# Cross-attention of a perceiver block: scores with the keys on the partitions

## The chip, the cores and the metric

The kernel runs on one core of one Trainium2 chip. The metric is the time of one execution on the device in microseconds (us). A core has five engines that run side by side, each through its own list in order: TensorE (PE: matmuls; weight loads are shown apart as PEld), VectorE (DVE), ScalarE (ACT), GpSimd (POOL), and SyncE (SP), which here only issues DMAs. They wait for each other through semaphores.

## The reference, cut to what matters

The block is a cross-attention, a self-attention and a mixture of experts, each with a layernorm before and a residual sum behind it. Only the first is touched:

```
x: (4, 256, 256)          ctx: (4, 4096, 256)
h       = layernorm(x)
queries = h @ Wq.T + bq
keys    = ctx @ Wk.T + bk
values  = ctx @ Wv.T + bv
scores  = einsum('bqc,bkc->bqk', queries, keys) / 16
attn    = softmax(scores, axis=-1)          # over 4096 keys
attended= einsum('bqk,bkc->bqc', attn, values)
x       = x + (h + attended) @ Wo.T + bo
```

All is float32.

## The kernel before, in words

The weights are folded: `qk` is h times (Wq.T Wk), so the scores are `qk` times the context itself, and the sum over keys mixes the raw context (`mix`); the value and output weights come behind it. A constant per query, `qbk`, remains of the biases. For accuracy each float32 operand of the large matmuls is split in a high part (a cast to fp32r) and a low part (the original less the high part), and three products are summed: high by high, low by high, high by low.

A batch has 256 queries (two tiles q of 128, `QT`) and 4096 keys, in eight chunks of 512 (`NCH`, `CH`; four tiles j of 128, `J`). The work is a pipeline of two stages over batches: in each of four passes the kernel computes the scores of one batch chunk by chunk, and beside them the probabilities and the mixing of the batch before. Pass 1 has only the first half, passes 2 to 4 have both, and a tail behind them has only the second. Pass 2 starts near 60 us, each full pass takes 65.9.

The list of each engine is written out by hand, by functions called once for each chunk c. In a chunk of a full pass:

- PE: `score` (12 matmuls of 512 columns, queries on the partitions of the result), `transpose_ctx` of the next chunk (8 transposes, L299), `mix` of the batch before (24 matmuls of 256 columns, L342 to L344), `transpose_probs` (8 transposes, L324).
- ACT: `ctx_turned_high` (casts the turned context to `ctxT_hi`, L494), `exps` (exponential of the stored scores, with the sum over keys as a by-product, L508), `probs_high` (casts turned probabilities to `pT_hi`, L517).
- DVE: `scores_out` (PSUM to SBUF, adds `qbk`, takes the maximum of the row as a by-product, L629), `ctx_low` (L614), `ctx_high` (casts the context as it came to `ctx_hi`, L622), `probs_low` (L637).
- POOL: `split`, the low part `ctx_lo` of the context as it came (L247). It needs `ctx_hi`. Its end frees one of four slots of `ctx_stage` for the load of the chunk four further on (L200, SP).

The maximum over all keys of a batch must be known before its first exponential, so `maxima` stands at the end of a pass; `invert_sums` and `normalise` close a batch. The queries of the next batch (`queries`), the product with the output weights (`product`), the statistics of the next layernorm and its scaling are spread over the chunks of a pass. The bias sum on `x_sb` (L261, POOL) is done once, in pass 2.

Of the kernel before, what the change touches and what calls it, by code (L numbers as in the profile page):

```python
# [100 lines left out]
def cross_attention(nc, x_sb, x_stats, x_mv, ident, kept, x, ctx, Wq, bq, Wk, bk, Wv, bv, Wo, bo,  # L101
# [3 lines left out]
    ATT_SCALE = 16 ** -0.5  # L105
    with ExitStack() as st:
# [122 lines left out]
        def _(pool):  # L229
            nc.gpsimd.memset(ident[:], 0.0).then_inc(ident_ok, 1)  # L230
            nc.gpsimd.memset(power[:], -0.5).then_inc(pow_g, 1)
# [8 lines left out]
            def split(b, c):  # L240
                cols = slice(c * J * D, (c + 1) * J * D)
# [5 lines left out]
                nc.gpsimd.tensor_tensor(ctx_lo[:, cols], ctx_in_sb[:, c % SLOTS, :], ctx_hi[:, cols].bitcast(F32),  # L247
                                        ALU.subtract).then_inc(split_g, 1)

            def second_scale(e):  # L250
                tiles = slice(QT * e, QT * (e + 1))
                pool.wait_ge(ve2_v, e + 1)
                nc.gpsimd.tensor_tensor(rstd2[:, tiles], ve2[:, tiles], power[:, tiles], ALU.pow).then_inc(rstd2_g, 1)

            for b in range(B):
                for c in range(NCH):
                    split(b, c)
                    if (b, c) == (1, 1):
# [1633 lines left out]
```

## Time and profile before

| | us |
|---|---|
| median of 3 runs | 674.49 (672.59 to 676.24) |
| the profiled execution | 672.18 |
| its span, first to last instruction | 670.4 |
| PE busy | 598.2 |
| DVE busy | 402.1 |
| ACT busy | 348.1 |
| POOL busy | 249.6 |
| mean granted TensorE clock | 0.964 of full |

A busy share is a mean over stages. A slice is a fortieth of the span, 16.8 us; a digit is its busy share in tenths. In a timeline a row gives the start, the time from start to end (of several instructions together, where it ends in x2 or more), engine, line, operation, result and inputs with their shapes, and in brackets the idle time of the engine before it and who ended it. Matmuls are pipelined: one is shown as 0.28 us long, while the next starts 0.12 later.

### The profile page before, as it was taken

How to read it: one execution, taken by the hardware profiler on the slowest of the kernel's cores; microseconds unless marked ns; L12 is line 12 of the kernel's file. 1: busy time of each engine (PE TensorE's matmuls, PEld its weight loads, DVE VectorE, ACT ScalarE, POOL GpSimd, SP SyncE). 2: the span in 40 equal slices, each digit the busy share in tenths (PEclk: the TensorE clock that was granted, in tenths of full speed). 3: DMA queues.
4: the chain of work that ended last, by engine and by line, in shares of the span. 5: the costliest groups of instructions: out<-in, count | busy, mean ns of one | idle time of the engine just before them, and what ended most of it. 6: DMA issues, size and time to landing. Idle time of an engine off the chain costs nothing. (4 is left out here: it accounts for less than half of the span.)

```text
span 670.4 us, 10668 instructions
## 1 busy us (share of the span) xinstructions
PE 598.2 (89%) x3740; PEld 475.4 (71%) x3740; DVE 402.1 (60%) x794; ACT 348.1 (52%) x1047; POOL 249.6 (37%) x201
## 2 busy tenths in 40 slices
PE   5998999999999998997887867999999876769998
PEld 4887998899989987975555546555558652448887
DVE  3766566666667664336477777699995378335000
ACT  2545444444444435632787861579996366751210
POOL 1352262233223232022696770133546149155000
PEclk8999999999999999999797999999999996699999
DMA  7122012102211220019993000300006147680000
GB/s 258 64 95 94 32 65 94 64 32 82 77 65 36 93 77 0 2 58 171 196 204 127 0 1 4 124 0 0 1 1 137 51 127 236 202 254 8 17 17 23
DMA packets 41586, 53.48 MB, mean 80 GB/s; under 512 B 3649, under 2 KB 37057, under 8 KB 41409
## 3 DMA queue, kind: packets, MB, share of 16 engines
q1 hardware_dynamic: 41536, 52.84, 28.7%
q8 instruction: 29, 0.48, 0.3%
q14 instruction: 21, 0.16, 0.1%
HBM read 48.63 MB, written 4.19 MB: 79 GB/s over the span
## 5 line engine op out<-in xcount | busy, mean ns | idle before, releaser
L247 POOL TENSOR_TENSOR ctx_lo<-ctx_stage,ctx_hi 128x1024 fp32r<-128x1024 f32 x32 | 76.3, 2387 | 157.3 <-DVE ctx_hi L622 135.8
L637 DVE TENSOR_TENSOR pT_lo<-ps,pT_hi 128x512 fp32r<-128x512 f32 x64 | 41.2, 686 | 60.0 <-ACT pT_hi L517 60.0
L342 PE MATMUL ps<-ctx_hi,pT_hi 128*128 128x256 f32 x256 | 75.2, 294 | 1.5 <-DVE pT_lo L637 1.4
L343 PE MATMUL ps<-ctx_lo,pT_hi 128*128 128x256 f32 x256 | 72.4, 283 | 0.0
L344 PE MATMUL ps<-ctx_hi,pT_lo 128*128 128x256 f32 x256 | 72.4, 283 | 0.0
L494 ACT CAST ctxT_hi<-ps 128x512 fp32r<-128x512 f32 x64 | 34.6, 593 | 62.7 <-PE ps L299 62.5
L1688 ACT ACTIVATE comb<-comb,cneg 128x64 f32<-128x64 f32 x160 | 62.9, 401 | 0.0
L629 DVE TENSOR_SCALAR_CACHE_REDUCE scores<-ps,qbk 128x512 f32<-128x512 f32 x64 | 47.5, 750 | 21.2 <-PE ps L311 21.2
L1574 PE MATMUL pf<-phiT,h3T 128*128 128x512 f32 x128 | 60.2, 591 | 0.0
L1659 PE MATMUL pf<-phiT,comb 128*128 128x256 f32 x256 | 56.2, 379 | 0.0
L508 ACT ACTIVATE probs<-scores,negmax 128x512 f32<-128x512 f32 x64 | 46.0, 728 | 16.3 <-DVE rowsum L648 16.3
L517 ACT CAST pT_hi<-ps 128x512 fp32r<-128x512 f32 x64 | 34.3, 589 | 36.6 <-PE ps L324 36.6
L1512 POOL TENSOR_TENSOR disp<-disp,dinv 128x512 f32<-128x512 f32 x32 | 33.6, 1049 | 52.7 <-DVE dinv L1765 52.7
L1659 PEld LDWEIGHTS pf<-phiT,comb 128*128 128x128 f32 x256 | 48.2, 190 | 6.8 <-issue 0.4
L342 PEld LDWEIGHTS ps<-ctx_hi,pT_hi 128*128 128x128 f32 x256 | 49.0, 191 | 2.4 <-DVE pT_lo L637 2.2
L343 PEld LDWEIGHTS ps<-ctx_lo,pT_hi 128*128 128x128 f32 x256 | 49.1, 192 | 0.1
L344 PEld LDWEIGHTS ps<-ctx_hi,pT_lo 128*128 128x128 f32 x256 | 49.0, 191 | 0.0
L614 DVE TENSOR_TENSOR ctxT_lo<-ps,ctxT_hi 128x512 fp32r<-128x512 f32 x64 | 41.2, 685 | 7.5 <-ACT ctxT_hi L494 7.1
L1523 POOL TENSOR_TENSOR comb<-comb,cinv 128x512 f32<-128x512 f32 x32 | 39.9, 1271 | 14.1 <-DVE cinv L1778 14.1
L311 PE MATMUL ps<-ctxT_hi,qk_hi 128*128 128x512 f32 x128 | 42.3, 411 | 2.8 <-issue 2.0
L311 PE MATMUL ps<-ctxT_hi,qk_lo 128*128 128x512 f32 x128 | 39.8, 392 | 0.0
L311 PE MATMUL ps<-ctxT_lo,qk_hi 128*128 128x512 f32 x128 | 39.7, 391 | 0.0
(204 smaller groups left out, 1368.3 us busy)
## 6 DMA issues: line engine op xcount, KB each, us to landing
ctx_stage<-in_ctx_dram SPq DMA_DIRECT2D x32, 512.0 KB, 3.3
w_more<-in_L_ffn_expert_w_dram SPq DMA_DIRECT2D x11, 1024.0 KB, 5.4
h3T<-in_L_ffn_expert_w_dram SPq DMA_DIRECT2D x5, 1024.0 KB, 5.3
qk_parts_dram<-qk_parts SPq DMA_DIRECT2D x8, 384.0 KB, 5.3
q_rows<-qk_parts_dram SPq DMA_DIRECT2D x24, 128.0 KB, 6.5
disp<-qk_parts_dram SPq DMA_DIRECT2D x24, 128.0 KB, 5.8
disp<-in_L_ffn_phi_w_dram SPq DMA_DIRECT2D x1, 2048.0 KB, 8.2
phiT<-in_L_ffn_expert_b_dram SPq DMA_DIRECT2D x4, 512.0 KB, 10.0
```

Of the source, the lines that this page charges most:

```text
L247: nc.gpsimd.tensor_tensor(ctx_lo[:, cols], ctx_in_sb[:, c % SLOTS, :], ctx_hi[:, cols].bitcast(F32), ALU.subtract).then_inc(split_g, 1)
L311: last = nc.tensor.matmul(pS[q][:], a[:, dh, q * P:(q + 1) * P], k[:, c % 2, dh, :], start=step == 0, stop=step == 5)
L342: nc.tensor.matmul(pO[q][:, 0:D], pT_hi[:, c % 2, q, cols], hi, start=c == 0 and j == 0, stop=False)
L343: nc.tensor.matmul(pO[q][:, 0:D], pT_hi[:, c % 2, q, cols], lo, start=False, stop=False)
L344: last = nc.tensor.matmul(pO[q][:, 0:D], pT_lo[:, c % 2, q, cols], hi, start=False, stop=c == NCH - 1 and j == J - 1)
L508: nc.scalar.activation(probs[:, c % 2, q, :], scores[:, q, c * CH:(c + 1) * CH], ACT.Exp, bias=negmax[:, q:q + 1], scale=SCALE, accum_out= ...
L614: nc.vector.tensor_tensor(ctxT_lo[:, c % 2, dh, :], ctx_banks(c, alone)[dh][:], ctxT_hi[:, c % 2, dh, :].bitcast(F32), ALU.subtract).then_ ...
L629: nc.vector.tensor_scalar(scores[:, q, c * CH:(c + 1) * CH], pS[q][:], qbk[:, b * QT + q:b * QT + q + 1], None, ALU.add, ALU.max, accum_ou ...
L637: nc.vector.tensor_tensor(pT_lo[:, c % 2, q, :], probs_banks(c, alone)[q][:], pT_hi[:, c % 2, q, :].bitcast(F32), ALU.subtract).then_inc(p ...
L1574: last = nc.tensor.matmul(psL[u % 4][:], hT[:, c, t * P:(t + 1) * P], phiT[:, c, cols], start=False, stop=c == DH - 1)
L1659: last = nc.tensor.matmul(psY[t][:, 0:HID], comb[:, t, s * P:(s + 1) * P], mixed[:, s, :], start=s == 0, stop=s == ST - 1)
L1688: nc.scalar.activation(column, column, ACT.Exp, bias=cneg[:, c, p:p + 1], accum_out=csum[:, c, p:p + 1]).then_inc(cslot_a, 1)
```

## The change

The scores are computed with the keys on the partitions: the turned context is the stationary operand and `qk` the moving one, four key tiles of 256 queries each, 24 matmuls of 256 columns in a chunk. The probabilities then come out in the layout in which `mix` takes them as the stationary operand, and `transpose_probs` goes.

The maximum over keys now runs over partitions. `running_maximum` (DVE, two of 512 elements a chunk, from PSUM) keeps the elementwise maximum in `running`; at the end of a pass `fold` halves it, `transpose_maxima` (PE) turns it, `shifts` (DVE) reduces it, adds `qbk` and takes the difference, and widens it; `spread_shift` (PE) and `shift_out` (ACT) lay the shift of each query along the free dimension of all partitions, as `shift`. Scores are copied to SBUF by ACT (`scores_out`, two copies of 512 a chunk, a ring of nine chunks in `turned_scores`). POOL adds the shift in place (`subtract`, 1024 elements a chunk). ACT takes the exponential in place (1024 elements) and casts it to `p_hi` (1024), and DVE takes `p_lo` from `turned_scores` and `p_hi`, both in SBUF (1024).

The sums over keys come from two columns of ones behind each 256 columns of `ctx_hi`, so that `mix` has 258 columns in two of three products, and `normalise` takes the reciprocal from PSUM. The PSUM banks are dealt out anew: two pairs for the scores, one for the turned context. `split` of a chunk is put off to two chunks later in POOL's list, and `mix` by one chunk in PE's.

The diff, cut to its core (`DE` is `D + 2`, `RING` is 9; it goes engine by engine, POOL, PE, ACT, DVE):

```
-        ctx_hi = sb("ctx_hi", [P, NCH * J * D], F32R)
+        ctx_hi = sb("ctx_hi", [P, NCH, J, DE], F32R)
-        scores = sb("scores", [P, QT, NCTX])
+        turned = sb("turned_scores", [P, RING, J * S])
...
+            def subtract(b, c):
+                m = NCH * b + c
+                pool.wait_ge(shift_a, b + 1)
+                part = turned[:, m % RING, :].rearrange("p (j q) -> p j q", j=J)
+                nc.gpsimd.tensor_tensor(part, part, shift[:].unsqueeze(1).broadcast_to([P, J, S]), ALU.add).then_inc(sub_g, 1)
-            for b in range(B):
+            for c in range(NCH):
+                split(0, c)
+            for b in range(1, B + 1):
                 for c in range(NCH):
-                    split(b, c)
+                    late = (b, c - 2) if c >= 2 else (b - 1, c + NCH - 2)
+                    if c and 0 < late[0] < B:
+                        split(*late)
+                    subtract(b - 1, c)
+                    if c == 0 and 0 < late[0]:
+                        split(*late)
                     if (b, c) == (1, 1):
...
...
             def score(b, c):
                 n = NCH * b + c
                 pe.wait_ge(ctxTlo_v, 2 * n + 2)
+                if c == 1:
+                    at_least(pe, shift_a, b)
...
+                for j in range(J):
...
-                    for a, k in ((qk_hi, ctxT_hi), (qk_lo, ctxT_hi), (qk_hi, ctxT_lo)):
+                    for k, a in ((ctxT_hi, qk_hi), (ctxT_hi, qk_lo), (ctxT_lo, qk_hi)):
                         for dh in range(DH):
-                            last = nc.tensor.matmul(pS[q][:], a[:, dh, q * P:(q + 1) * P], k[:, c % 2, dh, :],
+                            last = nc.tensor.matmul(score_banks(n)[j // 2][:, (j % 2) * S:(j % 2 + 1) * S],
+                                                    k[:, c % 2, dh, j * P:(j + 1) * P], a[:, dh, :],
                                                     start=step == 0, stop=step == 5)
...
+            def transpose_maxima(b):
+                to = score_banks(NCH * (b + 1) - 1)[0]
+                pe.wait_ge(fold_v, b + 1)
+                pe.wait_ge(scores_a, 2 * NCH * (b + 1))
                 for q in range(QT):
+                    last = nc.tensor.transpose(to[:, q * P:(q + 1) * P], running[:, q * P:(q + 1) * P], ident[:])
+            def spread_shift(b):
+                to = score_banks(NCH * (b + 1) - 1)[1]
+                pe.wait_ge(rowmax_v, 4 * (b + 1))
+                for q in range(QT):
+                    last = nc.tensor.matmul(to[:, q * P:(q + 1) * P], widened[:, q, :], ident[:], start=True, stop=True)
...
+            def scores_out(b, c):
+                n = NCH * b + c
+                at_least(act, plo_v, n - RING + 1)
+                for k in (1, 0):
+                    act.wait_ge(scores_mm, 2 * n + k + 1)
+                    if k == 0:
+                        act.wait_ge(max_v, 2 * n + 1)
+                    nc.scalar.copy(turned[:, n % RING, k * CH:(k + 1) * CH], score_banks(n)[k][:]).then_inc(scores_a, 1)
             def exps(b, c):
                 m = NCH * b + c
...
+                act.wait_ge(sub_g, m + 1)
+                nc.scalar.activation(turned[:, m % RING, :], turned[:, m % RING, :], ACT.Exp, scale=SCALE).then_inc(exp_a, 1)
...
+            def probs_high(b, c):
                 m = NCH * b + c
+                act.wait_ge(exp_a, m + 1)
+                at_least(act, pv_mm, m - 1)
+                nc.scalar.copy(p_hi[:, m % 2, :, :].rearrange("p j q -> p (j q)"), turned[:, m % RING, :]).then_inc(phi_a, 1)
             def batch(b):
+                for c in range(NCH):
+                    scores_out(b, c)
...
+                    exps(b - 1, c)
+                    probs_high(b - 1, c)
...
+            def probs_low(b, c):
                 m = NCH * b + c
+                dve.wait_ge(phi_a, m + 1)
+                nc.vector.tensor_tensor(p_lo[:, m % 2, :, :].rearrange("p j q -> p (j q)"), turned[:, m % RING, :],
+                                        p_hi[:, m % 2, :, :].rearrange("p j q -> p (j q)").bitcast(F32), ALU.subtract).then_inc(plo_v, 1)
             def batch(b):
                 for c in range(NCH):
-                    scores_out(b, c)
+                    running_maximum(b, c, 0)
+                    if c == 0:
+                        shifts(b - 1)
+                    running_maximum(b, c, 1)
                     if c < NCH - 1:
-                        ctx_low(b, c + 1, False)
+                        ctx_low(b, c + 1)
...
+                    probs_low(b - 1, c)
                     if c:
                         ctx_high(b, c - 1)
-                    if c < NCH - 1:
-                        probs_low(b - 1, c + 1, False)
```

In POOL's list, inside a full pass, only the split stood there before, with one small scaling in each pass:

```order
L247 TENSOR_TENSOR ctx_lo<-ctx_stage,ctx_hi 128x1024 [waits ctxT_mm,ctxhi_v] x8
L253 TENSOR_TENSOR rstd<-ve,power 128x2 [waits ve2_v]
L247 TENSOR_TENSOR ctx_lo<-ctx_stage,ctx_hi 128x1024 [waits ctxT_mm,ctxhi_v] x8
```

Now, in the middle of a full pass, split and shift alternate; `ctxhi_v` is counted up by DVE's `ctx_high`:

```order
L251 TENSOR_TENSOR turned_scores<-turned_scores,shift 128x1024 [waits shift_a]
L243 TENSOR_TENSOR ctx_lo<-ctx_stage,ctx_hi 128x1024 [waits ctxT_mm,ctxhi_v]
L251 TENSOR_TENSOR turned_scores<-turned_scores,shift 128x1024 [waits shift_a]
L243 TENSOR_TENSOR ctx_lo<-ctx_stage,ctx_hi 128x1024 [waits ctxT_mm,ctxhi_v]
L251 TENSOR_TENSOR turned_scores<-turned_scores,shift 128x1024 [waits shift_a]
```

Each shift has moved behind a split, and each split behind the shift of the chunk before.

In DVE's list, two chunks in the middle of a full pass, before (`probsThi_a` is counted up by ACT's `probs_high`):

```order
L614 TENSOR_TENSOR ctxT_lo<-ps,ctxT_hi 128x512 [waits ctxThi_a] x2
L622 CAST ctx_hi<-ctx_stage 128x1024 [waits pv_mm,ctx_in0]
L637 TENSOR_TENSOR pT_lo<-ps,pT_hi 128x512 [waits probsThi_a] x2
L629 TENSOR_SCALAR scores,cmax<-ps,qbk 128x512 [waits exp_a,scores_mm] x2
L614 TENSOR_TENSOR ctxT_lo<-ps,ctxT_hi 128x512 [waits ctxThi_a] x2
L622 CAST ctx_hi<-ctx_stage 128x1024 [waits pv_mm,ctx_in1]
L637 TENSOR_TENSOR pT_lo<-ps,pT_hi 128x512 [waits probsThi_a] x2
```

And now (`phi_a` is counted up by ACT's cast to `p_hi`):

```order
L649 TENSOR_TENSOR ctxT_lo<-ps,ctxT_hi 128x512 [waits ctxThi_a] x2
L695 TENSOR_TENSOR p_lo<-turned_scores,p_hi 128x1024 [waits phi_a]
L657 CAST ctx_hi<-ctx_stage 128x4x256 [waits pv_mm,ctx_in3]
L672 TENSOR_TENSOR running<-ps,running 128x512 [waits max_v,scores_mm]
L672 TENSOR_TENSOR running<-ps,running 128x512 [waits max_v,scores_a]
L649 TENSOR_TENSOR ctxT_lo<-ps,ctxT_hi 128x512 [waits ctxThi_a] x2
L695 TENSOR_TENSOR p_lo<-turned_scores,p_hi 128x1024 [waits phi_a]
L657 CAST ctx_hi<-ctx_stage 128x4x256 [waits pv_mm,ctx_in0]
```

The cast to `ctx_hi` stood in front of the low part of the probabilities of its chunk, and now stands behind it.

In ACT's list, one chunk in the middle of a full pass now (`sub_g` is counted up by POOL's shift):

```order
L532 COPY turned_scores<-ps 128x512 [waits scores_mm,plo_v]
L532 COPY turned_scores<-ps 128x512 [waits max_v,scores_mm]
L518 CAST ctxT_hi<-ps 128x512 [waits ctxT_mm,scores_mm]
L518 CAST ctxT_hi<-ps 128x512 [waits ctxT_mm]
L542 ACTIVATE turned_scores<-turned_scores 128x1024 [waits sub_g]
L548 CAST p_hi<-turned_scores 128x1024 [waits pv_mm,exp_a]
```

The two copies are new on ACT; the exponential and the cast are one instruction each, of 1024 elements, where there were two of 512.

## Rows read from the trace of the kernel before

**Rows 1.** The page: an engine's busy time, and its slices in tenths

```profile
PE 598.2 (89%) x3740; PEld 475.4 (71%) x3740; DVE 402.1 (60%) x794; ACT 348.1 (52%) x1047; POOL 249.6 (37%) x201
...
PE   5998999999999998997887867999999876769998
```

**Rows 2.** Timeline of POOL in pass 3: start, duration, engine, line, operation

```profile
148.13 2.40 POOL L247 TENSOR_TENSOR ctx_lo<-ctx_stage,ctx_hi 128x1024 fp32r<-128x1024 f32 x1 [4.98 <-DVE ctx_hi L622]
...
155.50 2.39 POOL L247 TENSOR_TENSOR ctx_lo<-ctx_stage,ctx_hi 128x1024 fp32r<-128x1024 f32 x1 [4.31 <-DVE ctx_hi L622]
```

**Rows 3.** Timeline of all engines, one chunk of pass 3

```profile
152.23 1.03 PE L299 MATMUL ps<-ident,ctx_stage 128*128 128x128 f32 x8
...
152.92 1.07 ACT L494 CAST ctxT_hi<-ps 128x512 fp32r<-128x512 f32 x2 [2.61 <-PE ps L299]
...
153.02 0.36 PE L342 MATMUL ps<-ctx_hi,pT_hi 128*128 128x256 f32 x1
...
153.54 1.29 DVE L614 TENSOR_TENSOR ctxT_lo<-ps,ctxT_hi 128x512 fp32r<-128x512 f32 x2 [0.23 <-ACT ctxT_hi L494]
...
154.74 0.68 DVE L622 CAST ctx_hi<-ctx_stage 128x1024 fp32r<-128x1024 f32 x1
...
155.97 1.04 PE L324 MATMUL ps<-ident,probs 128*128 128x128 f32 x8
...
156.77 0.70 PE L311 MATMUL ps<-ctxT_hi,qk_hi 128*128 128x512 f32 x2
```

**Rows 4.** Groups of instructions by shape: count, busy us, mean ns of one

```profile
L498 ACT CAST ctx_hi<-ctx_stage 128x1024 fp32r<-128x1024 f32 x8 | 8.4, 1064 | 0.0
...
L1682 ACT ACTIVATE disp<-disp 128x512 f32<-128x512 f32 x32 | 19.9, 622 | 3.4 <-DVE disp L1753 3.2
...
L1693 ACT ACTIVATE comb<-comb 128x2048 f32<-128x2048 f32 x3 | 5.7, 1900 | 0.0
...
L614 DVE TENSOR_TENSOR ctxT_lo<-ps,ctxT_hi 128x512 fp32r<-128x512 f32 x64 | 41.2, 685 | 7.5 <-ACT ctxT_hi L494 7.1
...
L644 DVE TENSOR_SCALAR negmax<-rowmax 128x2 f32<-128x2 f32 x4 | 0.7, 169 | 0.1
...
L261 POOL TENSOR_TENSOR x_sb<-x_sb,bo_all 128x2048 f32<-128x2048 f32 x1 | 4.6, 4622 | 0.0
```

**Rows 5.** Timelines of DVE and of POOL where both work, in three places

```profile
392.82 3.62 DVE L1339 TENSOR_TENSOR disp<-disp,phib 64x2048 f32<-64x2048 f32 x1
...
406.81 2.28 DVE L1339 TENSOR_TENSOR disp<-disp,phib 32x2048 f32<-32x2048 f32 x1
...
385.53 0.76 POOL L926 COPY v_pad<-v_all 128x64 f32 x4
...
392.41 1.89 POOL L934 TENSOR_TENSOR eB<-eB,rinv 128x1024 f32<-128x1024 f32 x1 [0.82 <-DVE rinv L1249]
394.25 2.82 POOL L926 COPY v_pad<-v_all 128x64 f32<-128x64 f32 x4
...
121.83 2.21 DVE L622 CAST ctx_hi<-ctx_stage 128x1024 fp32r<-128x1024 f32 x1 [0.82 <-PE ps L344]
...
121.09 2.39 POOL L247 TENSOR_TENSOR ctx_lo<-ctx_stage,ctx_hi 128x1024 fp32r<-128x1024 f32 x1 [6.97 <-DVE ctx_hi L622]
```

**Rows 6.** Timeline of PE, first scores of pass 2

```profile
59.58 0.70 PE L311 MATMUL ps<-ctxT_hi,qk_hi 128*128 128x512 f32 x2 [1.66 <-issue]
```

**Rows 7.** Timeline of PE: last matmul of the cross-attention, first behind it

```profile
290.87 0.28 PE L344 MATMUL ps<-ctx_hi,pT_lo 128*128 128x256 f32 x1
291.48 3.67 PE L982 MATMUL ps<-h2T,w_qkv 128*128 128x512 f32 x8 [0.33 <-PEq L106]
```

**Rows 8.** Stretches of 10 us: PE busy, granted clock, DMA share, GB/s

```profile
340.00:350.00 10.00, 8.15 (x88) 1.00 1.07 225
350.00:360.00 10.00, 5.72 (x46) 0.73 0.66 215
...
570.00:580.00 10.00, 7.32 (x48) 0.51 0.40 129
```

More of the change, by code:

```diff
@@ L105, in cross_attention @@
     ATT_SCALE = 16 ** -0.5
+    RING = 9
+    DE = D + 2
     with ExitStack() as st:
@@ L338, in mix @@
                     for j in range(J):
-                        hi = ctx_hi[:, (c * J + j) * D:(c * J + j + 1) * D]
-                        lo = ctx_lo[:, (c * J + j) * D:(c * J + j + 1) * D]
-                        cols = slice(j * P, (j + 1) * P)
-                        nc.tensor.matmul(pO[q][:, 0:D], pT_hi[:, c % 2, q, cols], hi, start=c == 0 and j == 0, stop=False)
-                        nc.tensor.matmul(pO[q][:, 0:D], pT_hi[:, c % 2, q, cols], lo, start=False, stop=False)
-                        last = nc.tensor.matmul(pO[q][:, 0:D], pT_lo[:, c % 2, q, cols], hi, start=False,
-                                                stop=c == NCH - 1 and j == J - 1)
+                        hi, lo = ctx_hi[:, c, j, :], ctx_lo[:, (c * J + j) * D:(c * J + j + 1) * D]
+                        rows = slice(q * P, (q + 1) * P)
+                        nc.tensor.matmul(pO[q][:, 0:DE], p_hi[:, m % 2, j, rows], hi, start=c == 0 and j == 0, stop=False,
+                                         skip_group_check=True)
+                        nc.tensor.matmul(pO[q][:, 0:D], p_hi[:, m % 2, j, rows], lo, start=False, stop=False, skip_group_check=True)
+                        last = nc.tensor.matmul(pO[q][:, 0:DE], p_lo[:, m % 2, j, rows], hi, start=False,
+                                                stop=c == NCH - 1 and j == J - 1, skip_group_check=True)
                 last.then_inc(pv_mm, 1)
@@ L656, in normalise @@
                 for q in range(QT):
+                    nc.vector.reciprocal(rinv[:, q:q + 1], pO[q][:, D:D + 1]).then_inc(rinv_v, 1)
+                for q in range(QT):
+                    dve.wait_ge(rinv_v, QT * b + q + 1)
                     nc.vector.tensor_scalar(att[:, q, :], pO[q][:, 0:D], rinv[:, q:q + 1], None, ALU.mult).then_inc(att_v, 1)
@@ L738, in _ @@
                     dve.wait_ge(weights_mm, BO_MM)
-                    nc.vector.tensor_tensor(bo_all[:], pO[1][:, 0:D], bo_all[:], ALU.add).then_inc(bo_v, 1)
+                    nc.vector.tensor_tensor(bo_all[:], pO[1][:, 0:D], bo_all[:], ALU.add).then_inc(small_v, 1)
                 if c == 3:
                     query_bias(1, QT, TT, pO[0])
-            maxima(0)
+            fold(0)
             dve.wait_ge(qbk_v, 2)
             queries_low(1)
-            ctx_low(1, 0, False)
             for b in range(1, B):
                 batch(b)
-            for c in range(NCH):
-                probs_low(LAST, c, True)
+            shifts(LAST)
+            probs_low(LAST, 0)
+            normalise(LAST - 1)
+            ctx_high(LAST, NCH - 1)
+            for c in range(1, NCH):
+                probs_low(LAST, c)
                 if c == 1:
```

320 lines of the change are left out of this document (155 added, 165 removed).

## The prediction

> **What bounds the kernel now.** I read the busy table first [rows 1]: TensorE (PE) 89% of the span, GpSimd (POOL) 37%, so work moved to POOL looks free. The slices then show where: up to about slice 18 (291 us) the tensor engine stands at 9 or 8 nearly without a break. That is the cross-attention, the only part that the change touches, so everything here is about when its last matmul ends: 290.87 us with the first matmul of the next stage at 291.48 [rows 7].
>
> The POOL timeline gives the beat of the steady state: ctx_lo starts at 148.13 and at 155.50 [rows 2], so one chunk of 512 keys costs 7.37 us, the same for every chunk inside a pass. The tensor engine's timeline shows what fills it [rows 3]: eight context transposes 152.23 to 153.02 (0.79), 24 mixing matmuls 153.02 to 155.97 (2.95, spaced 0.12), eight transposes of probabilities 155.97 to 156.77 (0.80), and the scores for the rest (2.83). No other engine is near it. POOL waits 4.98 us in a chunk for DVE's ctx_hi [rows 2], harmlessly.
>
> **The change on the tensor engine.** The eight probability transposes go: -0.80. The scores become 24 matmuls of 256 columns for 12 of 512; at the spacing of 0.12 of the mixing matmuls of that width [rows 3] this is 2.88 for 2.83, +0.05. Mixing goes to 258 columns in 16 of 24: two columns more, under 1%, +0.02. Sum 7.37 - 0.73 = 6.64 us. Were the engine still the bound, 24 chunks of passes 2 to 4 would give -17.5 us.
>
> **The other engines, per chunk.** ACT: four PSUM copies of 512 that issue every 0.49 (two take 1.07 [rows 3]) 2.0, one exponential of 1024 and one cast of 1024. Cast in the same form: 1.06 (L498). Exponential: 0.62 for 512 (L1682) and 1.90 for 2048 (L1693), so 1.05 for 1024 [rows 4]. Together 4.1. DVE: two maxima and two ctxT_lo at 0.69 as L614, one ctx_hi cast 0.68 [rows 3], and p_lo, 1024 elements with both inputs in SBUF: L614 has 0.685 for 512 (one input PSUM), L1339 2.28 for 2048 [rows 4, 5], so 1.22. Together 4.6. POOL: split 2.39, and the new shift. Its nearest row has the same form, a 256-wide row broadcast over blocks: L261, 4.62 for 2048 [rows 4], so 2.31 for 1024. Ends: 1.89 (L934, broadcast of single values) and 2.39 (L247). Together 4.7. All are under 6.64, and busy shares would say "faster".
>
> **What the order does.** Busy sums count only if the engines can run ahead of each other. The order rows say that they cannot. POOL: split of chunk c-1 stands in front of the shift of the next chunk of scores. That split waits for the cast ctx_hi. On DVE this cast now stands right behind p_lo of the current chunk, while before it stood in front of pT_lo. p_lo waits for ACT's p_hi, this for the exponential, and this for POOL's shift. So six instructions form a ring, one turn per chunk:
>
> shift 2.31, exponential 1.05, p_hi 1.06, p_lo 1.22, ctx_hi 0.60 (0.68 less the 0.08 by which it starts before its neighbour on DVE ends: 154.74 against 153.54 + 1.29 [rows 3]), split 2.39: 8.63. Handovers: from ctx_hi's end, 154.74 + 0.68, to POOL's start at 155.50 is 0.08; I take 0.09 for each of three between engines and 0.06 for the exponential to p_hi: 0.33. **8.96 us per chunk**, 1.59 more than before. ACT's copies and DVE's maxima fit into the 4.7 us in which POOL has the ring: from ctx_hi, a maximum 0.69, a score copy 0.5, two context copies 1.07, two ctxT_lo 1.29 make 3.6, and the scores then run 2.88 while ACT is at the exponential. PE is idle 2.3 us of each turn, in two gaps of about 1.
>
> **The whole of it**, from the first scores of pass 2, which before start at 59.58 [rows 6]:
> 1. To the end of the first shift: scores 2.9, transposing the folded maximum 0.3, then on DVE a reduction of 256 columns (0.42, by the slope of 1.04 ns an element between L614 and L1339) and two tiny ones (0.17 as L644 [rows 4], 0.25 with handover) and the widening (0.35), a matmul 0.5, a copy 0.6, shift 2.31: 8.0.
> 2. To the end of the third shift: pass 2 has no split behind its first shift, but the second exponential waits in ACT's order behind the copies of the next scores, and split 1 behind that: 14.5.
> 3. Five turns of the ring per pass, three passes: 15 x 8.96 = 134.4.
> 4. Twice from the last shift of a pass to the first of the next: e, p_hi, p_lo, ctx_hi 4.2, a maximum 0.69, the chain of step 1 from the reduction on, 2.2, shift 2.31: 9.45 each, 18.9.
> 5. The first two turns of passes 3 and 4: 10.15 (normalise adds 1.2 in front of ctx_hi) and 9.35 (statistics push p_lo by 0.4): 39.0.
> 6. Tail: 6.5 to the new shift, its subtraction 2.31, split 2.37, normalise and ctx_hi, split 2.39, a second shift until 18.95. From here POOL has only shifts. They collide with p_lo (below), so first p_lo at 21.3 to 22.5, then seven times 2.95 of mixing on PE and 3 x 0.4 of h2 transposes, with 2 for collisions: 46.5.
>
> Sum 261.3. One more term: in step 2 the bias addition to x_sb (4.62 on POOL) starts within 0.1 us of p_lo's request; half of 4.7 lost: 2.35. Total 263.7 against 290.87 + 0.28 - 59.58 = 231.6 before: +32.1. Pass 1 keeps its length (8 x 0.05 more for the scores); its last context transposes move ahead of the queries, and scores of pass 2 start some 0.6 earlier. The next stage gains two reciprocals, +0.3 at most. Net +31.8 on the profiled execution's 672.18 (span 670.4): 704.0 us. The median of the runs is 2.3 above that execution and their scatter +-1.8, which I leave in the range.
>
> **The collisions.** DVE's L1339, both inputs in SBUF, needs 3.62 us from 392.82 while POOL's L934 runs 392.41 to 394.30 [rows 5]; 394.2 + 2.28 is its end. Right after, POOL's four copies take 2.82 where four take 0.76 at 385.53. The ctx_hi cast at 121.83 takes 2.21 for 0.68, from under POOL's ctx_lo of 121.09 to 123.48. So such DVE work and POOL work exclude each other for whole instructions, while the maxima and ctxT_lo (one input from PSUM) go beside POOL: L614 has a mean of 0.685 over 64 that often lie beside ctx_lo. p_lo and ctx_hi are of the first sort. In the ring POOL happens to be idle then, so it costs nothing there; in the tail a turn becomes 2.31 + 1.22 = 3.5 if they alternate, and up to +8 if POOL goes first each time.
> The Trainium skill ("SBUF — State Buffer", Who interferes with whom) states this as an exclusive lock on a port pair, held for the whole instruction by a DVE instruction in a two-port mode or with two SBUF inputs; by that rule, the trace agrees, and it speaks against the change: p_lo used to read PSUM.
>
> **Rivals.**
> A, faster: POOL runs ahead, so the ring does not close and PE stays the bound. For it: all busy sums under 6.64. Against: the orders of POOL and DVE. It decides once the ring's sum falls below 6.64, that is if shift and split together took 2.4 instead of 4.7. Then 672.2 - 17.5 + 6 for the new waits at pass ends = 661. Chance 0.07.
> B, the ring with cheap shifts: 1.89 each instead of 2.31, 30 on the path, -12.6: 691. Chance 0.15.
> C, the ring and a falling tensor clock. In the attention stage PE at 8.15 busy of 10 keeps clock 1.00, and at 5.72 has 0.73; at 570 to 580, 7.32 busy, 0.51 [rows 8]. My ring has 6.64 of 8.96, 7.4 in 10. At mean 0.75 its work is 8.85 a turn and still just hidden, at 0.65 it is 10.2, +1.2 on 24: 704 + 29 = 733, but a PE fully busy regains the clock, so about half: 718. Chance 0.12.
> D, ctx_hi written into rows of 258 loses its fast mode (1.22 for 0.68) and handovers are 0.1 instead of 0.08: +0.65 on 24, with the tail at its upper end +4: 723. Chance 0.06.
> The ring as summed: 0.60, with 696 to 714 as its own range (0.3 us per turn either way).
>
> **Numbers.** 704.0, range 688 to 723. A change under 0.5% (3.4 us) could not be told from none: faster 0.07, same 0.02, slower 0.91.
>
> **What would show it.** POOL busy in that stage at about half, alternating ctx_lo and turned_scores, starts of ctx_lo 9.0 apart; POOL's ctx_lo waiting for DVE ctx_hi 4.3 us a turn, ACT's exponential waiting for POOL, PE's mixing matmuls waiting for p_lo about 1.3; PE busy near 74% there; the first matmul of the next stage near 323. A distance of 6.7 between ctx_lo starts would prove rival A; a shift of 1.9 us rival B; a granted clock under 0.9 between 70 and 300 us rival C; ctx_hi over 1.1 while POOL is idle rival D. It would be wrong altogether if POOL started a split before DVE's p_lo of the chunk in front had ended.

## The result, and the profile after

The changed kernel takes 716.13 us, median of 4 runs (715.45 to 718.84), for 675.37 before (672.59 to 676.68): ratio 1.0627, interval 1.0588 to 1.0666. It is slower by 41 us. The forecast was 704.0 with 688 to 723. The profiled execution took 715.47 us, its span 713.7. Medians and ranges in this document are over all runs of a kernel, while the ratios, with their 95% intervals, leave out one slow run each of three experiments (cast first, shift first, and ones early with shift first).

The page of the changed kernel, busy time and slices in tenths, answers to [rows 1]:

```profile
PE 602.3 (84%) x3892; PEld 489.1 (69%) x3892; DVE 403.0 (56%) x710; ACT 371.5 (52%) x987; POOL 324.1 (45%) x233
...
PE   6699888889878984869878886799999895789998
```

PE's row now stands mostly at 8 where 9 stood up to slice 18. Its first two slices, which before were 5 and 9, are 6 and 6 now; the larger part of my miss lies there, as will be seen.

The timeline of POOL in pass 2 (start, duration, engine, line, operation, and in brackets the wait ahead and who ended it) answers to [rows 2]:

```profile
97.76 2.38 POOL L251 TENSOR_TENSOR turned_scores<-turned_scores,shift 128x1024 f32<-128x1024 f32 x1
104.25 2.22 POOL L243 TENSOR_TENSOR ctx_lo<-ctx_stage,ctx_hi 128x1024 fp32r<-128x1024 f32 x1 [4.11 <-DVE ctx_hi L657]
106.41 2.40 POOL L251 TENSOR_TENSOR turned_scores<-turned_scores,shift 128x1024 f32<-128x1024 f32 x1
112.92 2.21 POOL L243 TENSOR_TENSOR ctx_lo<-ctx_stage,ctx_hi 128x1024 fp32r<-128x1024 f32 x1 [4.11 <-DVE ctx_hi L657]
```

Split and shift alternate, 8.66 us from one split to the next in the mean of a pass (8.67 in these rows), for 7.37 before. The rest of that turn, on ACT and DVE, then the waits of PE in it:

```profile
108.84 1.06 ACT L542 ACTIVATE turned_scores<-turned_scores 128x1024 f32<-128x1024 f32 x1 [2.41 <-POOL turned_scores L251]
109.93 1.05 ACT L548 CAST p_hi<-turned_scores 128x1024 fp32r<-128x1024 f32 x1
...
111.01 1.23 DVE L695 TENSOR_TENSOR p_lo<-turned_scores,p_hi 128x1024 fp32r<-128x1024 f32 x1 [3.76 <-ACT p_hi L548]
112.15 0.69 DVE L657 CAST ctx_hi<-ctx_stage 128x1024 fp32r<-128x1024 f32 x1
...
103.62 0.39 PE L362 MATMUL ps<-ctx_hi,p_hi 128*128 128x258 f32 x1 [0.95 <-DVE p_lo L695]
107.31 0.50 PE L325 MATMUL ps<-qk_hi,ctxT_hi 128*128 128x256 f32 x2 [0.53 <-DVE ctxT_lo L649]
```

Read it as a ring: the shift ends at 108.81, the exponential starts at 108.84, the cast at 109.93, p_lo at 111.01, ctx_hi at 112.15, the next split at 112.92. No instruction of it has slack in front of it; each waits for the one before. PE waits twice a turn.

The timelines of PE where the cross-attention begins, where pass 2 begins, and where the next stage begins, answer to [rows 6, 7]:

```profile
25.34 0.80 PE L325 MATMUL ps<-qk_hi,ctxT_hi 128*128 128x256 f32 x2 [5.44 <-DVE ctx_hi L775]
...
68.39 0.50 PE L325 MATMUL ps<-qk_hi,ctxT_hi 128*128 128x256 f32 x2 [1.08 <-DVE qk_lo L642]
...
332.30 0.28 PE L365 MATMUL ps<-ctx_hi,p_lo 128*128 128x258 f32 x1
332.91 1.52 PE L1034 MATMUL ps<-h2T,w_qkv 128*128 128x512 f32 x3 [0.33 <-PEq L108]
```

In the kernel before, the first of these stood at 19.46:

```profile
19.46 0.70 PE L311 MATMUL ps<-ctxT_hi,qk_hi 128*128 128x512 f32 x2 [0.36 <-issue]
```

With these marks the 43.3 us between the two spans (670.4 and 713.7) divide without a rest, here in us:

| stretch | before | after | difference | forecast |
|---|---|---|---|---|
| to the first scores of pass 1 | 19.46 | 25.34 | +5.9 | 0 |
| pass 1, to the first scores of pass 2 | 40.1 | 43.05 | +2.9 | -0.6 |
| passes 2 to 4, to the last mixing matmul | 231.6 | 264.2 | +32.6 | +32.1 |
| from there to the end of the span | 379.2 | 381.1 | +1.9 | +0.3 |

The part that I had worked out came out as a sum; the part that I had taken as unchanged did not.

**The start.** The timeline of DVE in the changed kernel shows what PE waited 5.44 us for:

```profile
20.12 1.29 DVE L649 TENSOR_TENSOR ctxT_lo<-ps,ctxT_hi 128x512 fp32r<-128x512 f32 x2 [1.39 <-ACT ctxT_hi L518]
21.32 3.89 DVE L628 TENSOR_SCALAR turned_scores<-x_sb,mv,rstd 128x256 f32<-128x256 f32 x6
25.17 0.11 DVE L775 MEMSET ctx_hi<- 128x64 f32 x1
```

The ones behind the values (L775, 0.11 us) are written behind six scalings of x, 3.89 us, and PE waits for the ones before its first scores, though they are read only by the mixing of pass 2. The scalings are themselves slowed: two of them take 0.73 where POOL has nothing (L628 at 7.56), so that six would take some 2.2, an estimate, while here POOL's first split runs from 21.59 to 23.76. The stretches around it (length, busy us of PE, PEld, DVE, ACT, POOL, then the granted clock, DMA share, GB/s) show a second price:

```profile
20.00:25.00 5.00, 0.00 (x0) 0.00 (x0) 4.88 (x8) 1.52 (x3) 2.17 (x1) 0.55 0.02 6
25.00:30.00 5.00, 4.66 (x22) 4.66 (x23) 0.98 (x3) 0.00 (x0) 0.00 (x0) 0.50 0.30 102
```

PE did nothing for 5 us, the granted clock fell to its lower level, 1.2 of 2.4 GHz, and stayed there for the first chunk's scores: from 25.34 to 30.63, where the same 24 matmuls take 2.9 us at the upper level.

**The tail.** POOL, then DVE, behind the last pass of scores:

```profile
303.62 1.61 POOL L256 TENSOR_TENSOR rstd<-ve,power 128x2 f32<-128x2 f32 x1 [2.98 <-DVE ve L723]
305.21 13.79 POOL L251 TENSOR_TENSOR turned_scores<-turned_scores,shift 128x1024 f32<-128x1024 f32 x5
...
312.32 2.05 DVE L695 TENSOR_TENSOR p_lo<-turned_scores,p_hi 128x1024 fp32r<-128x1024 f32 x1 [1.30 <-ACT p_hi L548]
314.29 4.86 DVE L730 TENSOR_SCALAR pT<-x_sb,x_mv,rstd 128x256 f32<-128x256 f32 x2
```

Five shifts take 2.76 each for 2.38 alone, and the two scalings of L730 take 4.86. The rstd of the layernorm (L256) stands in POOL's list between the shifts and waits 2.98 us for DVE. PE's waits in this stretch:

```profile
311.08 0.39 PE L362 MATMUL ps<-ctx_hi,p_hi 128*128 128x258 f32 x1 [2.40 <-DVE p_lo L695]
...
320.34 0.39 PE L362 MATMUL ps<-ctx_hi,p_hi 128*128 128x258 f32 x1 [2.82 <-DVE p_lo L695]
...
329.43 0.39 PE L362 MATMUL ps<-ctx_hi,p_hi 128*128 128x258 f32 x1 [1.11 <-DVE p_lo L695]
```

Ahead of all this PE waits 6.84 us for the last pass' shift to be worked out, and the clock falls once more (timeline of PE, then the stretch):

```profile
284.61 0.79 PE L346 MATMUL ps<-ident,pT 128*128 128x128 f32 x2 [6.84 <-DVE pT L690]
```

```profile
280.00:290.00 10.00, 5.39 (x25) 5.39 (x26) 2.78 (x6) 3.23 (x5) 3.68 (x2) 0.50 0.00 1
```

From the last pass' first shift on POOL (286.32) to the next stage are 46.6 us.

### The profile page after: what moved, and what is told of

It reads as the page before. It is cut to its first block and busy times, and to the rows that moved or that the text cites. A ratio compares the mean times of both kernels' runs of the same rounds, so it can differ in the third digit from the quotient of the medians.

```text
span 713.7 us, 10922 instructions
## 1 busy us (share of the span) xinstructions
PE 602.3 (84%) x3892; PEld 489.1 (69%) x3892; DVE 403.0 (56%) x710; ACT 371.5 (52%) x987; POOL 324.1 (45%) x233
## 5 line engine op out<-in xcount | busy, mean ns | idle before, releaser
L695 DVE TENSOR_TENSOR p_lo<-turned_scores,p_hi 128x1024 fp32r<-128x1024 f32 x32 | 39.9, 1251 | 97.2 <-ACT p_hi L548 97.2
L362 PE MATMUL ps<-ctx_hi,p_hi 128*128 128x258 f32 x256 | 78.1, 305 | 17.0 <-DVE p_lo L695 16.8
L251 POOL TENSOR_TENSOR turned_scores<-turned_scores,shift 128x1024 f32<-128x1024 f32 x32 | 78.5, 2459 | 28.4 <-ACT shift L537 28.4
L365 PE MATMUL ps<-ctx_hi,p_lo 128*128 128x258 f32 x256 | 74.4, 291 | 0.0
L364 PE MATMUL ps<-ctx_lo,p_hi 128*128 128x256 f32 x256 | 74.3, 290 | 0.0
L325 PE MATMUL ps<-qk_hi,ctxT_hi 128*128 128x256 f32 x256 | 55.9, 301 | 16.3 <-DVE ctxT_lo L649 6.7
L362 PEld LDWEIGHTS ps<-ctx_hi,p_hi 128*128 128x128 f32 x256 | 50.8, 199 | 21.0 <-DVE p_lo L695 21.0
L325 PE MATMUL ps<-qk_hi,ctxT_lo 128*128 128x256 f32 x256 | 53.4, 291 | 0.0
L325 PE MATMUL ps<-qk_lo,ctxT_hi 128*128 128x256 f32 x256 | 53.2, 291 | 0.0
L364 PEld LDWEIGHTS ps<-ctx_lo,p_hi 128*128 128x128 f32 x256 | 51.1, 200 | 0.1
L365 PEld LDWEIGHTS ps<-ctx_hi,p_lo 128*128 128x128 f32 x256 | 50.8, 198 | 0.0
```

The source lines that it names most:

```text
L251: nc.gpsimd.tensor_tensor(part, part, shift[:].unsqueeze(1).broadcast_to([P, J, S]), ALU.add).then_inc(sub_g, 1)
L325: last = nc.tensor.matmul(score_banks(n)[j // 2][:, (j % 2) * S:(j % 2 + 1) * S], k[:, c % 2, dh, j * P:(j + 1) * P], a[:, dh, :], start=s ...
L362: nc.tensor.matmul(pO[q][:, 0:DE], p_hi[:, m % 2, j, rows], hi, start=c == 0 and j == 0, stop=False, skip_group_check=True)
L364: nc.tensor.matmul(pO[q][:, 0:D], p_hi[:, m % 2, j, rows], lo, start=False, stop=False, skip_group_check=True)
L365: last = nc.tensor.matmul(pO[q][:, 0:DE], p_lo[:, m % 2, j, rows], hi, start=False, stop=c == NCH - 1 and j == J - 1, skip_group_check=True)
L695: nc.vector.tensor_tensor(p_lo[:, m % 2, :, :].rearrange("p j q -> p (j q)"), turned[:, m % RING, :], p_hi[:, m % 2, :, :].rearrange("p j ...
```

## The experiments

Times are medians beside the kernel before (675.49 in the first four, 675.18 in the last three). The third and fourth columns are in us, from the profiled executions: the distance of POOL's ctx_lo starts inside a pass, and the time from pass 2's first scores to the next stage's first matmul. The last has its 95% interval in brackets.

| kernel | time, us | ctx_lo apart | passes 2 to 4 | ratio to before |
|---|---|---|---|---|
| before | 675 | 7.37 | 231.9 | |
| changed | 716.1 | 8.66 | 264.5 | 1.0627 |
| ones early | 706.5 | 8.66 | 264.5 | 1.0439 (1.0358 to 1.0521) |
| cast first | 698.2 | 7.36 | 246.1 | 1.0344 (1.0256 to 1.0432) |
| shift first | 695.4 | 6.3 to 6.6 | 243.5 | 1.0243 (1.0114 to 1.0371) |
| tiny shift | 666.9, one run | 6.47 to 6.64 | 219.4 | |
| ones early, shift first | 687.6 | 6.3 to 6.6 | 243.5 | 1.0207 (1.0111 to 1.0302) |
| shift on DVE, ones early | 667.7 | 6.6 | 224.4 | 0.9892 (0.9815 to 0.9968) |
| shift twice | 789.1, one run | 11.1 | 335.3 | |

**Ones early.** The one line of L775 at the head of DVE's list.

```
+ nc.vector.memset(ctx_hi[:, :, :, D:DE].bitcast(F32), 1.0).then_inc(ones_v, 1)
  dve.wait_ge(x_in[0], 16)
  first_statistics(0, QT)
  ...
  first_norm(QT, TT)
- nc.vector.memset(ctx_hi[:, :, :, D:DE].bitcast(F32), 1.0).then_inc(ones_v, 1)
```

> The changed kernel with the memset of the columns of ones moved from behind the first layernorm's scaling to the head of DVE's list. Ring theory (the excess over the forecast is one wait at the start: PE's first scores wait for the ones, queued on DVE behind six scalings, and then run at half clock; the ring of six instructions is untouched): first scores at about 19.9 us instead of 25.3, starts of ctx_lo still 8.66 apart, 716 becomes 709 (707 to 711). Rival (pass 1 is slow because ACT now copies the scores too): first scores early, but those of pass 2 still near 68, time 715 to 717.

Measured: 706.51 (705.14 to 707.65), 9.6 below the changed kernel and a little below the 707 to 711 expected. PE's first scores stand right behind the transposes, and pass 2 begins 5.75 us earlier:

```profile
20.38 1.07 PE L309 MATMUL ps<-ident,ctx_stage 128*128 128x128 f32 x8 [0.47 <-DVE qk_lo L642]
21.20 0.48 PE L325 MATMUL ps<-qk_hi,ctxT_hi 128*128 128x256 f32 x2
...
62.64 0.51 PE L325 MATMUL ps<-qk_hi,ctxT_hi 128*128 128x256 f32 x2 [1.08 <-DVE qk_lo L642]
```

Passes 2 to 4 keep 264.5 to a tenth, so the start and the ring are separate losses. Of the 8.7 us between the two spans 5.8 are in this part; the other 2.9 lie behind the cross-attention, where the kernels are the same and where spans of one program scatter.

**Cast first.** DVE issues the ctx_hi cast ahead of p_lo, which takes exponential, p_hi and p_lo out of the ring.

```
- probs_low(b - 1, c)
  if c:
      ctx_high(b, c - 1)
- elif b >= 2:
+ probs_low(b - 1, c)
+ if c == 0 and b >= 2:
      normalise(b - 2)
      ctx_high(b - 1, NCH - 1)
```

> The changed kernel with DVE's cast to ctx_hi in front of p_lo in each chunk from the second of a pass on, as it stood before the change. No instruction is added or removed. Ring theory: the split no longer hangs on p_lo, the ring is open, a chunk costs what PE needs, 6.7 to 7.0 us instead of 8.66; about 20 chunks, time 672 to 685, most likely 677. Rival (POOL's added work as such costs, or the exclusion between POOL and DVE): POOL and DVE do the same instructions, a chunk stays at 8 us or above, time 700 to 716. Rival (a falling tensor clock): no change.

Measured: 698.17 (692.0 to 703.22), well above the 672 to 685 that I expected. The turn is 7.36, neither the ring's nor PE's. DVE and POOL in pass 3 show why:

```profile
178.57 0.69 DVE L657 CAST ctx_hi<-ctx_stage 128x1024 fp32r<-128x1024 f32 x1 [0.20 <-PE ps L365]
179.78 2.85 DVE L695 TENSOR_TENSOR p_lo<-turned_scores,p_hi 128x1024 fp32r<-128x1024 f32 x1 [0.51 <-ACT p_hi L548]
```

```profile
179.35 2.20 POOL L243 TENSOR_TENSOR ctx_lo<-ctx_stage,ctx_hi 128x1024 fp32r<-128x1024 f32 x1 [1.79 <-DVE ctx_hi L657]
181.51 3.39 POOL L251 TENSOR_TENSOR turned_scores<-turned_scores,shift 128x1024 f32<-128x1024 f32 x1
```

p_lo is issued under the split (until 181.55) and ends 1.08 us behind its end, at 182.63; the shift issued there ends at 184.90, 2.27 behind p_lo's end. Each waits for the other's whole instruction, so p_lo costs 2.85 for 1.23 and the shift 3.39 for 2.38. And a ring is closed again: ctx_hi to split 0.78, split 2.20, from there to the end of p_lo 1.08, and 3.29 for PE's mixing, which waits for p_lo and for which the next ctx_hi waits: 7.35. This handover between DVE and POOL is in no order of instructions; I had the exclusion as a rival (a chunk at 8 us or above) and not in my sum. The Trainium skill ("SBUF — State Buffer", Who interferes with whom), named in the prediction, says that a DVE instruction with two SBUF inputs contends with a GpSimd instruction that reads SBUF; the trace agrees, with p_lo at 2.85 for 1.23.

**Shift first.** POOL issues the shift ahead of the delayed split.

```
- if c and 0 < late[0] < B:
-     split(*late)
  subtract(b - 1, c)
- if c == 0 and 0 < late[0]:
+ if 0 < late[0] < B or (c == 0 and 0 < late[0]):
      split(*late)
```

> The changed kernel with POOL's shift of a chunk in front of the delayed split instead of behind it; DVE as in the changed kernel. Ring theory: the next shift no longer waits for a split that waits for p_lo, so the ring is open at another place; what remains is the sum of what excludes each other on POOL and DVE, 2.20 + 2.38 + 1.23 + 0.69 = 6.5 us, close to PE's 6.64: 6.7 to 7.3 a chunk, time 675 to 692, most likely 682. Rival (POOL's amount of work costs): a chunk at 8 us or above, 700 to 716.

Measured: 695.42 (688.37 to 698.81), 13 above the most likely value and 3 above the range, though inside a pass the turn is PE's (13.00 us busy of 13 from 108 to 121 us). POOL from one pass into the next:

```profile
181.52 2.20 POOL L243 TENSOR_TENSOR ctx_lo<-ctx_stage,ctx_hi 128x1024 fp32r<-128x1024 f32 x1 [2.07 <-DVE ctx_hi L655]
183.68 2.41 POOL L251 TENSOR_TENSOR turned_scores<-turned_scores,shift 128x1024 f32<-128x1024 f32 x1
188.14 2.19 POOL L243 TENSOR_TENSOR ctx_lo<-ctx_stage,ctx_hi 128x1024 fp32r<-128x1024 f32 x1 [2.05 <-DVE ctx_hi L655]
200.32 2.39 POOL L251 TENSOR_TENSOR turned_scores<-turned_scores,shift 128x1024 f32<-128x1024 f32 x1 [9.99 <-ACT shift L535]
```

6.62 from split to split, and then 9.99 us of waiting, since the shift of a pass is known only when all its scores are. From the first shift of this pass (134.01) to that of the next a pass takes 66.3 us, where eight turns of 6.6 make 53: 13.5 over. In the changed kernel it is 72.2 us (141.88 to 286.32 for two) for 69.3, 2.9 over: there the slow turns hid the border. I had expected the ring's loss back whole and got it less what came out from under it. The tail keeps its five shifts in 13.79 us.

**Tiny shift.** The shift works on 2 elements instead of 1024, so the scores are not shifted.

```
- nc.gpsimd.tensor_tensor(part, part, shift[:].unsqueeze(1).broadcast_to([P, J, S]), ALU.add)
+ nc.gpsimd.tensor_tensor(part[:, 0, 0:2], part[:, 0, 0:2], shift[:, 0:2], ALU.add)
```

> The changed kernel, where POOL's shift handles 2 elements of a partition instead of 1024, so the scores are not shifted before the exponential; all orders and waits as in the changed kernel. Ring theory: the ring loses 2.38 less the 0.15 that a tiny instruction takes, 8.66 becomes about 6.5, below what PE needs, so PE bounds again at 6.65 to 6.8 a chunk; the tail loses the collisions too: time 662 to 672. Rival (clock or the new form of the matmuls): a chunk above 7.5, time above 690.

Measured: 666.86 in one run, with late ones and all. The ring is there, but POOL's part of it is a split and 0.2:

```profile
93.30 2.21 POOL L243 TENSOR_TENSOR ctx_lo<-ctx_stage,ctx_hi 128x1024 fp32r<-128x1024 f32 x1 [4.12 <-DVE ctx_hi L657]
95.45 0.21 POOL L251 TENSOR_TENSOR turned_scores<-turned_scores,shift 128x2 f32<-128x2 f32 x1
99.77 2.21 POOL L243 TENSOR_TENSOR ctx_lo<-ctx_stage,ctx_hi 128x1024 fp32r<-128x1024 f32 x1 [4.12 <-DVE ctx_hi L657]
```

6.47 apart: 8.66 less 2.19, where the shift went from 2.38 to 0.21, 2.17 less. PE had no gap in this stretch (16.00 us busy of 16 from 90 to 106), so ring and PE are about equally long here; later in the pass, at 6.61 to 6.63, POOL waits 4.26 to 4.28 and PE sets the turn.

**Shift twice.** The other direction: POOL adds the shift two times.

```
+ nc.gpsimd.tensor_tensor(part, part, shift[:].unsqueeze(1).broadcast_to([P, J, S]), ALU.add).then_inc(twice_g, 1)
+ pool.wait_ge(twice_g, m + 1)
  nc.gpsimd.tensor_tensor(part, part, shift[:].unsqueeze(1).broadcast_to([P, J, S]), ALU.add).then_inc(sub_g, 1)
```

> POOL adds the shift twice to every chunk (the scores are shifted twice). Theory (POOL's shift lies in the closed ring with no slack): a turn grows by the whole instruction and its semaphore, 2.38 + 0.06, to 11.1 us, and all 32 shifts lie on the path: 716 + 32 x 2.44 = 794 (788 to 798). Rival (another engine or the falling clock shares the bound, the ring has slack): less than 1.5 us a turn, under 765.

Measured: 789.11 in one run. Splits 11.14 apart, 2.48 above the changed kernel, the whole of a shift and its semaphore:

```profile
103.99 2.19 POOL L244 TENSOR_TENSOR ctx_lo<-ctx_stage,ctx_hi 128x1024 fp32r<-128x1024 f32 x1 [4.11 <-DVE ctx_hi L660]
106.14 2.40 POOL L252 TENSOR_TENSOR turned_scores<-turned_scores,shift 128x1024 f32<-128x1024 f32 x1
108.62 2.40 POOL L254 TENSOR_TENSOR turned_scores<-turned_scores,shift 128x1024 f32<-128x1024 f32 x1
115.13 2.20 POOL L244 TENSOR_TENSOR ctx_lo<-ctx_stage,ctx_hi 128x1024 fp32r<-128x1024 f32 x1 [4.11 <-DVE ctx_hi L660]
```

The other turns of this pass are 11.09 to 11.13. POOL still waits 4.11 for ctx_hi: no slack took any of it. Passes 2 to 4 grow by 70.8 us, for the 78 that 32 times 2.44 make: inside the passes the shift counts whole, at the borders of passes and in the tail not all of it (from the last pass' first shift to the next stage 60.4 for 46.6, 13.8 for eight shifts).

**Ones early and shift first.** Both edits as above.

```
+ nc.vector.memset(ctx_hi[:, :, :, D:DE].bitcast(F32), 1.0).then_inc(ones_v, 1)   # DVE, first
...
  subtract(b - 1, c)                                                              # POOL
+ if 0 < late[0] < B or (c == 0 and 0 < late[0]):
      split(*late)
```

> Both edits at once: the ones are written at the head of DVE's list, and POOL's shift stands in front of the delayed split. Theory (two separate losses, the start of pass 1 and the ring): the gains add, so from the 695.4 with the shift first alone minus the 9.6 that the early ones were worth: 686 (682 to 690), ctx_lo starts still 6.3 to 6.6 apart inside a pass, pass boundaries still 12 us. Rival (one loss hides the other: pass 2 waits for POOL and DVE anyway, so an earlier pass 1 is eaten by the first shifts): within 3 us of 695.

Measured: 687.61 (682.41 to 693.36), 7.8 below the shift first alone, with passes 2 to 4 at 243.5 in both. The two gains add, within the scatter of these runs, which is wider than that of the changed kernel.

**Shift on DVE.** DVE does the shift, one chunk ahead of the exponential, and POOL only the split; the ones are early. All of the reference is computed.

```
- subtract(b - 1, c)       # POOL
...
  def batch(b):            # DVE; the same in the tail
      ...
+     if c == 0:
+         subtract(b - 1, 0)
+     if c < NCH - 1:
+         subtract(b - 1, c + 1)
      probs_low(b - 1, c)
```

> The same mathematics with the shift on DVE (1.22 us as p_lo takes, for 2.38 on POOL), always one chunk ahead of the exponential, and the early ones; POOL keeps only the split. Theory (the price of the change is the ring through POOL; the arithmetic itself fits under PE): DVE has 5.8 us a chunk, POOL 2.2, so PE's 6.5 us a chunk sets the beat, as in the kernel with the tiny shift, 666.9, less 9.6 for the start: 657 (653 to 668), below the kernel before the change. DVE's shift, p_lo and ctx_hi and POOL's split exclude each other, 1.22 + 1.22 + 0.6 + 2.2 = 5.3 us, still under 6.5. Rival (DVE with 5.8 of 6.5 and the exclusion becomes the bound): 7.3 us a chunk or more, 680 or more.

Measured: 667.74 (665.09 to 669.16), ratio 0.9892 to the kernel before, interval 0.9815 to 0.9968, a gain of about 1%: the only version that computes everything and beats both. It is still 11 above the 657 I expected, at the edge of what I allowed (668). DVE in pass 2:

```profile
101.77 1.22 DVE L689 TENSOR_TENSOR turned_scores<-turned_scores,shift 128x1024 f32<-128x1024 f32 x1
103.09 1.22 DVE L694 TENSOR_TENSOR p_lo<-turned_scores,p_hi 128x1024 fp32r<-128x1024 f32 x1
104.23 0.69 DVE L650 CAST ctx_hi<-ctx_stage 128x1024 fp32r<-128x1024 f32 x1
```

The same shift takes 1.22 us here for 2.38 on POOL, and PE is without a gap inside a pass (30.00 busy of 80 to 110 us). What is left of the price is at the borders of passes, in POOL's timeline:

```profile
111.64 2.19 POOL L243 TENSOR_TENSOR ctx_lo<-ctx_stage,ctx_hi 128x1024 fp32r<-128x1024 f32 x1 [4.44 <-DVE ctx_hi L650]
119.43 2.20 POOL L243 TENSOR_TENSOR ctx_lo<-ctx_stage,ctx_hi 128x1024 fp32r<-128x1024 f32 x1 [5.60 <-DVE ctx_hi L650]
130.58 2.18 POOL L243 TENSOR_TENSOR ctx_lo<-ctx_stage,ctx_hi 128x1024 fp32r<-128x1024 f32 x1 [8.96 <-DVE ctx_hi L650]
140.86 2.20 POOL L243 TENSOR_TENSOR ctx_lo<-ctx_stage,ctx_hi 128x1024 fp32r<-128x1024 f32 x1 [8.09 <-DVE ctx_hi L650]
```

7.79, 11.15 and 10.28 for 6.6. From 130.58 to 193.34, where the next pass stands at the same place, are 62.8 us for 8 x 6.6, 10.0 over; in the kernel before, 65.9 for 8 x 7.37 (140.76 to 206.63), 6.9 over. So of the 6.2 that eight turns gain a pass keeps 3.1. In the tail, DVE's scaling is without POOL's shifts beside it what I used above:

```profile
271.44 0.73 DVE L729 TENSOR_SCALAR pT<-x_sb,x_mv,rstd 128x256 f32<-128x256 f32 x2
```

and from the last pass' first shift (247.20) to the next stage are 38.3 us, for 46.6.

## Why the prediction was right, and where it was not

The median, 716, lies in the range, but above the 696 to 714 of the ring as summed and close to the 718 of rival C. The number alone would have spoken for C; the rows below do not.

**The ring was right, in kind and in size.** Forecast 8.96 us a turn, measured 8.66. From start to start, with what I had: shift 2.43 (2.40), exponential 1.09 (1.11), p_hi 1.08 (1.15), p_lo 1.14 (1.22), ctx_hi 0.77 (0.69), split 2.16 (2.39). The split is most of the difference: I took its 2.39 over, but reading ctx_hi from rows of 258 it takes 2.20. That the shift lies in a closed ring is shown by the two experiments on its length: 2.17 less gives 2.19 less a turn, 2.48 more gives 2.48 more. That the other five lie in it is read from the rows, where each starts within 0.1 us of the end of the one before, and the two changes of order, which shortened the turn without taking any work away, bear it out; none of the five was varied by itself. Rival A (POOL runs ahead) falls with the same rows, and with POOL's wait of 4.11 for ctx_hi (forecast 4.3). Rival B needed a shift of 1.9; it took 2.38, so the row of the same form [rows 4] was the right neighbour for it. Rival C: the granted clock in the steady state stayed 1.00 (100 to 140 us and 168 to 203 us), so it did not lengthen the turn. Outside it the sign that I had named for C did show: 0.66 in 75 to 80 and in 150 to 155 us, 0.50 in 280 to 290. What that cost at the borders of passes was not taken apart. Rival D: ctx_hi kept 0.69. PE's busy share was 8.2 of 10 in 100 to 140 us, for the forecast 7.4. Its waits in a turn are 0.95 for p_lo and 0.53 for ctxT_lo, 1.5 together for the 2.3 forecast. The shorter turn explains 0.3 of this; the rest was not taken apart, and a part of it is how the profile shows matmuls, the last one ahead of a gap as 0.28 long where the next could start after 0.12.

**The step that failed was "Pass 1 keeps its length".** It was a sentence about the length of pass 1, and I asked nothing about its start. PE's new wait for the ones stands in the code that I had before me, and so does the place of the memset at the end of DVE's list. To name what stands ahead of the thing waited for would have given it: six scalings, 3.89 us. At the start of pass 2 I was 9.4 us low (68.39 for 59.0): 5.9 by the later start, 2.4 by scores at the lower clock, 1.1 by the rest of pass 1, in which the clock fell again. The run with ones early and shift first, whose granted clock stayed 1.00 all through pass 1, bears this out: its pass 1 took 39.9 us (18.25 to 58.16), for the 39.5 forecast. The early ones brought the start of pass 2 forward by 5.75 in the traces and the median down by 9.6, of the 12.1 by which the forecast was low. (The first scores stand at 24.1 to 26.7 in five executions with the late ones, at 18.1 to 21.2 in three with the early ones, so single traces leave a scatter of 2 to 3 us here.)

**The tail was sized too small:** 53.1 us (from 279.47 to 332.58) for 46.5, with 2 us in it for collisions. Up to the end of the first p_lo behind normalise, at 301.75, it went as summed: 22.3 for 21.3 to 22.5. The seven mixings behind it, which I had at 2.95 each with 1.2 for transposes and the 2 for collisions, took 30.8 for 24. The rows show where: PE waited 2.40, 0.19, 2.82 and 1.11 for p_lo, and the mixing from 320.34 to 324.85 took 4.5, at a granted clock of 0.66 in 320 to 325.

- "From here POOL has only shifts" was wrong. L256 stands among them: POOL waited 2.98 for its input and then needed 1.61 for it (0.70 inside a pass). The shift behind it came late by as much, and so did the p_lo for which PE waited 2.40.
- The collisions were the mechanism I named, but the instruction that they hit hardest was not in my list: second_norm, L730, 4.86 for 0.73, ahead of the p_lo for which PE waited 2.82.
- The last exponential stands on ACT behind a copy (L558) that waited 6.69 for the transposes behind the slow mixing; this is the wait of 1.11.

The first mixing of the tail, at the lower clock from 285.48 with 24 groups at 0.21 for 0.12 us, did not count: the work on DVE that needs it stood behind a p_lo until 292.13, and that one waited for ACT. No run took the three terms apart. The version without shifts on POOL shows only that all of it, with the shifts themselves, is worth 8.3 (46.6 to 38.3); there L730 took 0.73.

**Terms that cancelled.** From the end of a pass' third shift to the end of its last, the five turns took 43.45, 43.50 and 43.43, in sum 130.4 for 134.4. Steps 1, 4 and 5 came out within 1 us each. Step 2 was 14.2 for 14.5 + 2.35: p_lo slipped in front of the bias addition at 79.44, and it was POOL that waited, 5.62 for 4.62. So passes 2 to 4 came out at 264.2 for 263.7 by a ring that was 4.0 too long, a step 2 that was 2.6 too long and a tail 6.6 too short: nearly exact as a sum, by luck, and not in its terms.

## What to carry to other kernels

When a change makes work cheaper on the busiest engine and adds it on idle ones, follow one turn of the loop through every engine's own order; if it closes, its sum is the bound, whatever the shares of busy time say. Here the same arithmetic costs 41 us or gains 7, by which engine does one addition and where one memset of 0.11 us stands. Of each added wait ask not only who gives it but what stands ahead of that in its engine's list, above all for work of no size.

## What the runs showed of the hardware that I had not expected

- PE's granted clock fell to 0.50 in the middle of full work, not only after idle time. In the changed kernel, PE busy 5.00 of 5.00:

```profile
50.00:55.00 5.00, 5.00 (x33) 5.00 (x31) 1.14 (x3) 0.96 (x2) 1.70 (x1) 0.66 0.33 106
```

  With the ones early the same is seen at 44 to 50 us (0.80, 0.50, 0.84), with the shift on DVE 0.56 in 42 to 48. Before the change it was 1.00 there. The score matmuls are of 256 columns for 512 and loads of weights go with them without a gap (PEld 5.00 of 5.00). That alone is not the cause: with the tiny shift, and with ones early and shift first, the same matmuls ran at 1.00 from 36 us to the end of pass 1 (profiled executions, one of each). What it is stays open. It costs some 1.7 us (0.72 as the mean of 50 to 56 us).
- Two GpSimd additions of 1024 elements in float32, both from SBUF, took 2.20 (split out of rows of 258) and 2.38 (in place, a row of 256 broadcast). The split out of contiguous rows before took 2.39 [rows 2]. In pass 1, where no shift runs, the split takes 2.17 to 2.20 too. The layout of its operands is what changed in it, and the difference is 0.19 us an instruction; no run changed the layout by itself.
- DVE work that only reads and writes SBUF (p_lo with two inputs there, the scaling L730 with one and two values a partition) and GpSimd's additions take turns by whole instructions when both are always ready: in the tail five shifts at 2.76 each, DVE's small scaling of 256 elements at 2.4 each for 0.4. A short instruction pays for the long one of its neighbour each time, so it is short DVE work that is to be kept away from long POOL work.
